# Reordering the first forty microseconds of a two-layer attention block on one core: norms, halves of x, values and queries, and the loads of the biases

## The chip, the core and the metric

The kernel runs on one core of one Trainium2 chip. The metric is the device time of one execution, in microseconds (us); lower is better. All arithmetic that matters is in float32. Matrix products are made from pairs of numbers, a high part (type fp32r) and a low part that holds the rest, with three matmuls for each product: high by high, high by low and low by high.

## What is computed

There are 32 sequences of 128 tokens with 512 features. Two layers of the same form run one after the other, each on the output of the one before. In short, for each sequence:

```
xn = layernorm(x) * norm_scale + norm_bias
q, k, v = xn @ Wq + bq, xn @ Wk + bk, xn @ Wv + bv      # 512 x 512 weights
k, v = masked(k), masked(v)
q = softmax(q, over the features of a head)             # 16 heads, then 8
k = softmax(k, over the tokens)
y = q @ (k.T @ v)                                       # linear attention, by head
scale, shift = split(silu(cond) @ W_film + b_film)
h = layernorm(y) * film_scale + film_bias, times (1 + scale), plus shift
x = x + silu(h) @ Wo + bo
```

## The kernel before

The x of all 32 sequences stays on chip (tile X, one slot of 128x512 for each sequence). A "tile" below is one sequence in one layer, so there are 64 of them; two neighbours, tiles 2g and 2g+1, are a pair g. Every engine has its own hand-written list of steps, which it works through strictly in order, and each step starts with waits on semaphores that other engines' steps raise. After the first few tiles the lists become a loop over tiles, step(s); the order of the steps before it is written out call by call, and the change is in that part alone. The calls that it touches:

- Weights. A 512x512 matrix is loaded in four chunks of 128 rows. `split_high(w, [c])` on ScalarE (ACT) copies chunk c of weight w into the high part; `split_low(eng, w, [c])` subtracts to get the low part (L346), on VectorE (DVE) or on GpSimd (POOL) depending on whose list it stands in. Weights 0 to 3 are Wk, Wv, Wq and Wo of the first layer. `keys(0)`, `values(0)` and `queries(0)` on TensorE (PE) wait chunk by chunk for these low parts.
- Norms. `stat_x(n)` on DVE takes mean and variance of tile n (L1515, L1518) and waits for the load of X where tile n is the first of a load. `root_x(n)` on POOL makes the reciprocal root. `norm_x(n)` on DVE (for tiles 0 to 3) writes the normalised tile XN (L1526).
- Turning. `turn_x(m)` on PE transposes half of the features of a pair (m = 2g + half) into PSUM; its first half waits for both tiles of the pair. `x_turned(m)` on ACT takes it out with the norm's scale and bias (two instructions at L935) and makes the high part XH (L942). `x_low(m)` makes the low part XL (L1563). The scale and bias lie in VC, which `start_vectors` on DVE copies (L1778) from what `turn_vectors` on PE transposed.
- Products. `keys(i)`, `values(i)`, `queries(i)` on PE are 24, 12 and 12 matmuls (L1152). Each waits until DVE has emptied the PSUM bank of the tile before: `queries(1)` waits for the first instruction of DVE's `queries(0)` (L1608), `values(1)` for DVE's `values(0)` (L1620). DVE's `queries(i)` also takes the maximum by head (L1612); then POOL's `queries(i)` subtracts it (L658), and then DVE's `turn_queries(i)` turns the result into QS (L1547).
- Filling. `keep_busy(b, n)` on PE makes n products of the identity with itself that nobody reads; each shows as two instructions in the profile.
- Loads. SyncE (SP) issues the large loads one after the other into one queue: `load_x(n)` (load 2 is tiles 2 and 3, load 3 tiles 4 to 7, load 4 tiles 8 to 11), `load_w(w)` (1 MB), `load_bias(r)` (a row of 512 numbers for all 128 partitions; 0 is bv, 1 bq, 2 bo) and `load_film(n)` (2 MB). `wait_split(1)` holds SP until the low parts of Wv are made, since load 4 goes into the place where Wv was staged.

Later in the opening, after DVE's `stat_x(5)` and `stat_x(6)`, DVE's list goes on with `start()`, `start_cond()` (L1756), `x_low(2)`, `x_low(3)`, `start_valid()` (L1748, L1749). PE's `turn_cond()` waits for `start_cond()`, PE's `count()` (L1351) for `start_valid()`, and `keys(2)` stands behind both.

Of the kernel before, what the change touches and what calls it, by code (L numbers as in the profile page):

```python
# [44 lines left out]
def build_blocks(nc, x, cond, mask0, mask1, weights, film_w, vec_rows, bias_rows, out):  # L45
# [21 lines left out]
    with ctx:  # L67
# [84 lines left out]
        B_K, B_V, B_Q, B_XK, B_O, B_TY, B_Y = 0, 1, 2, 3, 4, 5, 6  # L152
# [63 lines left out]
        def placed_x(g):  # L216
            return 16 * Q * ((g - FIRST) // 2 + 1)
# [123 lines left out]
        def split_low(eng, w, chunks):  # L341

            for c in chunks:
                wait_weights(eng, w, c)
                eng.wait_ge(act_w, C * w + c + 1)
                eng.tensor_tensor(WL[w % 4][:, c, :], STAGES[w][:, c, :], WH[w % 4][:, c, :].bitcast(F32),  # L346
                                  ALU.subtract).then_inc(low_w[w][c], 1)
# [26 lines left out]
        def _(eng):  # L374
# [4 lines left out]
            def load_w(w):  # L379
                src = weights[0][w].rearrange("(c p) n -> p c n", p=P)  # L380
                eng.dma_start(STAGES[w][:, :, :], src).then_inc(ld_w[w - 1], 16)
# [17 lines left out]
            def load_bias(r):  # L399
                eng.dma_start(BB[:, r, :], bias_rows[r:r + 1].partition_broadcast(P)).then_inc(ld_bias[r], 16)  # L400
# [101 lines left out]
            load_first(eng, [1])  # L502
            load_x(2)
            load_w(1)
            load_bias(2)
            load_bias(0)
            load_bias(1)
            load_w(2)
            load_film(0)
            load_x(3)  # L510
            wait_split(1)
# [89 lines left out]
        def _(eng):  # L601
# [16 lines left out]
            def root_x(n):  # L618
                eng.wait_ge(dve_stat, n + 1)
                r = n % RING  # L620
                if n - RING >= 2 * FIRST:
                    eng.wait_ge(act_xn, n - RING - 2 * FIRST + 1)
                if n < 2 * FIRST:
                    root(MVX[:, r, 1:2], VEX[:, :], RSX[:, r:r + 1]).then_inc(pool_x, 1)
                else:
                    root(MVX[:, r, 1:2], VEX[:, :], RSX[:, r:r + 1]).then_inc(pool_own, 1)
                    own[0] += 1
                    eng.wait_ge(pool_own, own[0])
                    eng.tensor_scalar(NBX[:, r:r + 1], MVX[:, r, 0:1], RSX[:, r:r + 1], -1.0, ALU.mult, ALU.mult)\  # L629
                       .then_inc(pool_x, 1)  # L630
                eng.wait_ge(pool_x, n + 1)
# [62 lines left out]
            mask_of_keys(0)  # L694
            root_x(2)
            root_x(3)
            split_low(eng, 2, [0])
            normalise_keys(0)
            queries(0)
# [112 lines left out]
        def _(eng):  # L812
            def split_high(w, chunks=range(C)):

                if w in LAST_USE:
                    eng.wait_ge(LAST_USE[w], B)
                for c in chunks:
                    wait_weights(eng, w, c)
                    eng.activation(WH[w % 4][:, c, :], STAGES[w][:, c, :], ACT.Copy).then_inc(act_w, 1)
# [98 lines left out]
            def x_turned(m):  # L918

                g, p = divmod(m, 2)  # L920
                l = g // (B // 2)
                if g < FIRST:
                    eng.wait_ge(pe_a, m + 1)
                elif p == 0:
                    eng.wait_ge(ld_xt[g % 2], placed_x(g))
                if g == 0 and p == 0:
                    eng.wait_ge(dve_vec, 1)
                wait_x_low(eng, m - 1 if m <= 2 * FIRST else m)
                xf = XF1 if m in (1, 3) else XF0[:, :, :]
                for cc in range(2):  # L930
                    if g < FIRST:
                        src = PS[:, B_X[p], cc * PAIR:(cc + 1) * PAIR].rearrange("p (t q n) -> p t q n", t=2, q=Q)
                    else:
                        src = XT[:, :, :, 2 * p + cc, :].rearrange("p q t n -> p t q n")
                    f = eng.activation(xf[:, cc, :].rearrange("p (t q n) -> p t q n", t=2, q=Q), src, ACT.Identity,  # L935
                                       bias=vec(l, "norm_bias", 2 * p + cc, 1),
                                       scale=vec(l, "norm_scale", 2 * p + cc, 1))
                f.then_inc(act_xf, 1)
                eng.wait_ge(act_xf, m + 1)
                if g >= 2:  # L940
                    eng.wait_ge(pe_q, 2 * g - 2)
                eng.activation(XH[g % 2][:, 2 * p:2 * p + 2, :], xf, ACT.Copy).then_inc(act_xh, 1)  # L942
# [24 lines left out]
            eng.dma_start(MI, mask0).then_inc(ld_mask, 16)  # L967
            eng.dma_start(MF, mask1).then_inc(ld_mask, 16)
            split_high(0, [0])
            split_high(0, [1])  # L970
            split_high(0, [2])
            split_high(0, [3])
            x_turned(0)
            x_turned(1)
            split_high(1, [0])
            split_high(1, [1])
            cond_tanh()
# [160 lines left out]
        def _(eng):  # L1138
            def bank(b, a=0, n=512):
                return PS[:, b, a:a + n]  # L1140
# [43 lines left out]
            def values(i):  # L1184
                eng.wait_ge(dve_v, i)
                project_x(i, 1, bank(B_V), pe_v)
# [109 lines left out]
            def turn_x(m):  # L1296
                g, p = divmod(m, 2)
                if m >= 2:
                    eng.wait_ge(act_xf, m - 1)
                for t in range(2):  # L1300
                    if p == 0:
                        eng.wait_ge(dve_xn, m + t + 1)
                    for cc in range(2):
                        f = (2 * p + cc) * P
                        mm = eng.transpose(bank(B_X[p], cc * PAIR + t * T, T), XN[:, t, f:f + P], ident[:, :])
                mm.then_inc(pe_a, 1)
# [29 lines left out]
            def turn_vectors():  # L1336

                eng.wait_ge(pool_const, 4)
                eng.wait_ge(ld_vec, 16)
                n = 2 * VROWS  # L1340
                eng.transpose(bank(B_TY, 0, n), VR, ident[0:n, 0:n]).then_inc(pe_vec, 1)

            def keep_busy(b, n):

                for _ in range(n):
                    eng.matmul(bank(b, 0, P), ident[:, :], ident[:, :], start=True, stop=True)
# [13 lines left out]
            def turn_valid():  # L1360

                eng.wait_ge(dve_mask_rows, 1)
                for l in range(2):
                    mm = eng.transpose(bank(B_O, (EC + l) * B, B), MT if l == 0 else MF, ident[0:B, 0:B])
                mm.then_inc(pe_valid, 1)

            eng.wait_ge(pool_const, 2)
            keep_busy(B_Q, 4)
            keep_busy(B_Q, 6)
            turn_x(0)  # L1370
            turn_vectors()
            turn_x(1)
            keep_busy(B_Q, 2)
            keep_busy(B_Q, 2)
            keep_busy(B_Q, 2)
            keep_busy(B_Q, 2)
            keep_busy(B_Q, 2)
            keep_busy(B_Q, 2)
            keep_busy(B_Q, 2)
            keys(0)  # L1380
            keys(1)
            keep_busy(B_Q, 2)
            turn_x(2)
            turn_valid()
            queries(0)
            values(0)
            queries(1)
            turn_x(3)
            values(1)
            turn_cond()  # L1390
            count()
            keys(2)
# [107 lines left out]
        def _(eng):  # L1500
# [20 lines left out]
            def norm_x(n):  # L1521
                g, t = divmod(n, 2)
                eng.wait_ge(pool_x, n + 1)
                if g > 0:
                    eng.wait_ge(pe_a, 2)
                eng.tensor_scalar(XN[:, t, :], X[:, n % B, :], MVX[:, n % RING, 0:1], RSX[:, n % RING:n % RING + 1],  # L1526
                                  ALU.subtract, ALU.mult).then_inc(dve_xn, 1)
# [55 lines left out]
            def key_sums(i):  # L1583

                eng.wait_ge(act_ek, i + 1)
                eng.wait_ge(pool_kn, i)
                eng.reciprocal(RE[:, :], SE[:, i % 2, :]).then_inc(dve_re, 1)  # L1587
# [187 lines left out]
            def start_vectors():  # L1775

                eng.wait_ge(pe_vec, 1)
                eng.tensor_copy(VC[:, :], PS[:, B_TY, 0:2 * VROWS]).then_inc(dve_vec, 1)  # L1778

            stat_x(0)  # L1780
            stat_x(1)
            norm_x(0)
            split_low(eng, 0, [0])
            norm_x(1)
            split_low(eng, 0, [1])
            split_low(eng, 0, [2])
            start_vectors()
            split_low(eng, 0, [3])
            stat_x(2)
            stat_x(3)  # L1790
            x_low(0)
            x_low(1)
            split_low(eng, 1, [0])
            start_masks()
            norm_x(2)
# [2 lines left out]
            keys(0)  # L1798
            split_low(eng, 2, [1])
            split_low(eng, 2, [2])  # L1800
            split_low(eng, 1, [3])
            split_low(eng, 2, [3])
            split_low(eng, 1, [1])
            keys(1)
            key_sums(0)
            queries(0)
            stat_x(4)
            values(0)
            turn_queries(0)
            stat_x(5)  # L1810
            stat_x(6)
# [232 lines left out]
```

## Time and profile before

| what | value |
|---|---|
| time, median of 3 executions | 863.16 us (862.21 to 863.73) |
| span of the profiled execution | 861.2 us |
| median less that span (what lies around the profiled instructions) | 1.96 us |
| busy PE, PE weight load, DVE, ACT, POOL | 98%, 84%, 79%, 70%, 64% |

The profile gives the start and length of every instruction of one execution, in us from the start of its span. Of an engine's list it shows what ended an idle time (in brackets, behind an arrow). The chain of work that ended last is followed back from the last instruction: at each step to what released it, or to the instruction ahead of it on its engine. DMA rows give the time from issue to landing. The granted clock (PEclk) is the share of TensorE's full speed, 1.00 for 2.4 GHz and 0.50 for 1.2 GHz.

### The profile page before, as it was taken

Reading aid. Unit: us, or ns where it says so; the run is one execution under the profiler, and the core shown is the slowest. Engines: PE = TensorE matmul, PEld = TensorE weight load, DVE = VectorE, ACT = ScalarE, POOL = GpSimd, SP = SyncE. Lnnn points to the kernel's source line nnn. Section 1 sums busy time; section 2 is a strip of 40 time slices with the busy share of each in tenths; the row PEclk is TensorE's granted clock in tenths of the full one; section 3 lists DMA queues with packets and bytes.
Section 4 is the critical chain, followed back from the end, with each engine's and each line's share of the span. In section 5 each row is a group of like instructions: output and inputs, shape, how many; then the busy total and the mean of one; then the engine's idle time right before and its main releaser. Section 6 shows DMA issues by size and latency. Waiting matters only on the chain.

```text
span 861.2 us, 20095 instructions
## 1 busy us (share of the span) xinstructions
PE 842.2 (98%) x6659; PEld 720.4 (84%) x6659; DVE 679.9 (79%) x1362; ACT 602.7 (70%) x1442; POOL 548.8 (64%) x741
## 2 busy tenths in 40 slices
PE   7999999999999999999999999999999999999998
PEld 7778888888888888888877888888888888888886
DVE  6987778778788778778887887778778777787666
ACT  5377677677676776677777786776676676676665
POOL 3467765765765756766767767667667656765641
PEclk8999999999999999999999999999999999999999
DMA  9876676776776766656578656656566655667441
GB/s 304 286 221 207 190 230 189 226 226 192 201 216 197 227 208 185 178 167 180 168 232 235 194 176 185 208 181 203 167 197 199 201 187 185 177 192 206 145 159 62
DMA packets 139404, 169.81 MB, mean 197 GB/s; under 512 B 12302, under 2 KB 112006, under 8 KB 139302
## 3 DMA queue, kind: packets, MB, share of 16 engines
q1 hardware_dynamic: 138512, 167.56, 64.0%
q8 instruction: 53, 0.87, 0.4%
q10 hardware_dynamic: 790, 0.98, 0.4%
q14 instruction: 49, 0.40, 0.2%
HBM read 95.61 MB, written 72.88 MB: 196 GB/s over the span
## 4 chain that ended last, share of the span: by engine, by line
PE 76%; DMA 9%; DVE 4%; SPq 3%; issue 3%; ACT 3%; POOL 2%; DVEq 0%; ACTq 0%; POOLq 0%
PE PS L1152 65%; PE PS L1248 6%; PE PS L1232 3%; DMA k_turned<-KT 2%; DMA X<-in_x 2%; DMA QT<-qy_turned 2%; DMA EK<-k_turned 1%; DMA qy_turned<-QS 1%; SPq L438 1%; DMA XT<-x_turned 1%; SPq L459 1%; PE PS L1322 1%; ACT Z L867 1%; POOL XL L667 1%; ACT XF L935 0%
## 5 line engine op out<-in xcount | busy, mean ns | idle before, releaser
L680 POOL TENSOR_TENSOR HL<-H,HH 128x512 fp32r<-128x512 f32 x60 | 77.4, 1290 | 190.1 <-ACT HH L916 190.0
L867 ACT ACTIVATE Z<-QT,FC,FA 128x128 f32<-128x128 f32 x240 | 99.0, 483 | 92.0 <-DMA QT<-qy_turned 92.0
L1152 PE MATMUL PS<-XH,WH_k 128*128 128x256 f32 x512 | 149.7, 292 | 0.7 <-DVE KN L1581 0.7
L1152 PE MATMUL PS<-XH,WL_k 128*128 128x256 f32 x512 | 144.7, 283 | 0.0
L1152 PE MATMUL PS<-XL,WH_k 128*128 128x256 f32 x512 | 144.7, 283 | 0.0
L953 ACT ACTIVATE XN<-X,NBX,RSX 128x512 f32<-128x512 f32 x60 | 48.8, 813 | 86.6 <-POOL NBX L629 86.6
L829 ACT ACTIVATE SK<-SK,KN 128x128 f32<-128x128 f32 x256 | 98.9, 388 | 11.2 <-DVE KN L1581 11.2
L1152 PE MATMUL PS<-WH_o,HH 128*128 128x512 f32 x248 | 102.3, 413 | 3.4 <-issue 3.2
L1152 PE MATMUL PS<-WH_q,XH 128*128 128x512 f32 x256 | 100.7, 394 | 0.0
L1152 PE MATMUL PS<-WH_v,XH 128*128 128x512 f32 x256 | 100.7, 394 | 0.0
L1152 PE MATMUL PS<-WL_v,XH 128*128 128x512 f32 x256 | 100.3, 392 | 0.0
L1152 PE MATMUL PS<-WL_q,XH 128*128 128x512 f32 x256 | 99.8, 390 | 0.0
L1152 PE MATMUL PS<-WH_q,XL 128*128 128x512 f32 x256 | 99.7, 389 | 0.0
L1152 PE MATMUL PS<-WH_v,XL 128*128 128x512 f32 x256 | 99.6, 389 | 0.0
L1152 PEld LDWEIGHTS PS<-XH,WH_k 128*128 128x128 f32 x512 | 97.8, 191 | 1.3 <-issue 1.1
L1152 PE MATMUL PS<-WL_o,HH 128*128 128x512 f32 x248 | 98.1, 395 | 0.0
L1152 PEld LDWEIGHTS PS<-XL,WH_k 128*128 128x128 f32 x512 | 97.9, 191 | 0.1
L1152 PE MATMUL PS<-WH_o,HL 128*128 128x512 f32 x248 | 98.0, 395 | 0.0
L1152 PEld LDWEIGHTS PS<-XH,WL_k 128*128 128x128 f32 x512 | 97.8, 191 | 0.0
L651 POOL TENSOR_TENSOR X<-X,BB 128x512 f32<-128x512 f32 x64 | 83.7, 1309 | 0.2
L667 POOL TENSOR_TENSOR XL<-XF,XH 128x512 fp32r<-128x512 f32 x60 | 78.1, 1301 | 5.5 <-issue 4.2
L674 POOL TENSOR_TENSOR SK<-SK,RE 128x512 f32<-128x512 f32 x64 | 66.6, 1041 | 19.6 <-DVE RE L1587 19.4
(171 smaller groups left out, 2108.3 us busy)
## 6 DMA issues: line engine op xcount, KB each, us to landing
qy_turned<-QS SPq DMA_DIRECT2D x60, 512.0 KB, 2.9
QT<-qy_turned SPq DMA_DIRECT2D x240, 128.0 KB, 3.1
EK<-k_turned SPq DMA_DIRECT2D x128, 128.0 KB, 2.8
x_turned<-XS SPq DMA_DIRECT2D x30, 512.0 KB, 3.3
XT<-x_turned SPq DMA_DIRECT2D x120, 128.0 KB, 3.5
k_turned<-KT SPq DMA_DIRECT2D x52, 256.0 KB, 3.9
out_x<-X SPq DMA_DIRECT2D x31, 256.0 KB, 3.3
X<-in_x SPq DMA_DIRECT2D x11, 512.0 KB, 5.3
```

The source lines that it names most:

```text
L438: eng.dma_start(QT[32 * fq:32 * fq + 32, :, 0:n, :, :].rearrange("p q h c n -> p q (h c n)"), src[fq])\
L459: eng.dma_start(EK[32 * tq:32 * tq + 32, :, :, :, :, :].rearrange("p f h t c n -> p f (h t c n)"), src[tq])\
L651: eng.tensor_tensor(X[:, b, :], X[:, b, :], BB[:, 2, :], ALU.add).then_inc(pool_bo, 1)
L667: eng.tensor_tensor(XL[g % 2][:, dst, :], XF0[:, :, :], XH[g % 2][:, dst, :].bitcast(F32), ALU.subtract).then_inc(pool_xl, 1)
L674: eng.tensor_tensor(sk, sk, RE[:, :].unsqueeze(2).to_broadcast([P, 4, T]), ALU.mult).then_inc(pool_kn, 1)
L680: eng.tensor_tensor(hl_of(o), h_of(o), hh_of(o).bitcast(F32), ALU.subtract).then_inc(pool_hl, 1)
L829: e = eng.activation(SK[:, p, a, :], SK[:, p, a, :], ACT.Exp, bias=KN[:, p, t, cc:cc + 1], accum_out=SE[:, p, a:a + 1])
L867: z = eng.activation(z_of(o)[:, c * P:c * P + P].rearrange("p (q n) -> p q n", q=Q), src, ACT.Identity, bias=FC[l][:, c, b:b + 1], scale=F ...
L953: eng.activation(XN[:, t, :], X[:, n % B, :], ACT.Identity, bias=NBX[:, r:r + 1], scale=RSX[:, r:r + 1]).then_inc(act_xn, 1)
L1152: mm = eng.matmul(dst, left[a](c), right[b](c), start=(c == 0 and a + b == 0), stop=(c == C - 1 and a == 1))
L1232: mm = eng.matmul(PS[f:f + 32, bank_att(j), c * P + a:c * P + a + w], vs if l == 0 else ks, ks if l == 0 else vs, start=True, stop=True, t ...
L1248: mm = eng.matmul(bank(B_Y + c // 2, (c % 2) * W, W), EQ[:, c * P:c * P + P], ATT[:, c // 2, (c % 2) * W:(c % 2 + 1) * W], start=True, sto ...
```

## The change

No step is added or removed except fillers of PE; steps stand at other places of the lists, and two low parts move from DVE to POOL.

- SP: Wq is loaded ahead of the three biases, and these come in the order bv, bq, bo (before: bo, bv, bq, then Wq).
- POOL: chunks 1 and 3 of Wv's low part are made here, ahead of Wq's chunk 0.
- ACT: `x_turned(0)` follows the first chunk of Wk and `x_turned(1)` the second (before: both after all four).
- PE: `turn_vectors()` comes before `turn_x(0)`; `values` come before `queries` for tiles 0 and 1, and `turn_x(3)` comes after `values(1)`; ahead of `keys(0)` 9 filler products stand where 14 stood, and the 2 after `keys(1)` are gone.
- DVE: `start_vectors` and `norm_x(1)` come ahead of the first low part of Wk; `x_low(0)`, `x_low(1)` and `stat_x(2)` come between its chunks; two chunks of Wv are gone; and the order behind `key_sums(0)` is `values(0)`, `stat_x(4)`, `queries(0)` (before: `queries(0)`, `stat_x(4)`, `values(0)`).

```diff
@@ SP
             load_w(1)
-            load_bias(2)
+            load_w(2)
             load_bias(0)
             load_bias(1)
-            load_w(2)
+            load_bias(2)
             load_film(0)
             load_x(3)
@@ POOL
             root_x(3)
+            split_low(eng, 1, [1])
+            split_low(eng, 1, [3])
             split_low(eng, 2, [0])
@@ ACT
             split_high(0, [0])
+            x_turned(0)
             split_high(0, [1])
+            x_turned(1)
             split_high(0, [2])
             split_high(0, [3])
-            x_turned(0)
-            x_turned(1)
@@ PE
             eng.wait_ge(pool_const, 2)
-            keep_busy(B_Q, 4)
-            keep_busy(B_Q, 6)
+            keep_busy(B_Q, 10)
+            turn_vectors()
             turn_x(0)
-            turn_vectors()
             turn_x(1)
-            keep_busy(B_Q, 2)
...
+            keep_busy(B_Q, 9)
             keys(0)
             keys(1)
-            keep_busy(B_Q, 2)
             turn_x(2)
+            values(0)
             turn_valid()
             queries(0)
-            values(0)
+            values(1)
+            turn_x(3)
             queries(1)
-            turn_x(3)
-            values(1)
             turn_cond()
@@ DVE
             norm_x(0)
+            start_vectors()
+            norm_x(1)
             split_low(eng, 0, [0])
-            norm_x(1)
+            x_low(0)
             split_low(eng, 0, [1])
+            stat_x(2)
+            x_low(1)
             split_low(eng, 0, [2])
-            start_vectors()
             split_low(eng, 0, [3])
-            stat_x(2)
             stat_x(3)
-            x_low(0)
-            x_low(1)
             split_low(eng, 1, [0])
...
             split_low(eng, 2, [2])
-            split_low(eng, 1, [3])
             split_low(eng, 2, [3])
-            split_low(eng, 1, [1])
             keys(1)
             key_sums(0)
+            values(0)
+            stat_x(4)
             queries(0)
-            stat_x(4)
-            values(0)
             turn_queries(0)
```

## Rows read from the trace of the kernel before

**Rows 1.** The page: busy time by engine, then the whole chain by engine.

```profile
PE 842.2 (98%) x6659; PEld 720.4 (84%) x6659; DVE 679.9 (79%) x1362; ACT 602.7 (70%) x1442; POOL 548.8 (64%) x741
...
PE 76%; DMA 9%; DVE 4%; SPq 3%; issue 3%; ACT 3%; POOL 2%; DVEq 0%; ACTq 0%; POOLq 0%
```

**Rows 2.** The chain in order of time, 18 to 60: start, length, what.

```profile
10.84 18.50 DMA X<-in_x
...
29.37 0.70 DVE BNX L1515
...
30.92 0.70 DVE QS L1547
...
35.40 0.81 DVE XL L1563 x2
...
36.86 0.41 PE PS L1351 x2
37.26 2.95 PE PS L1152 x24
40.22 1.85 PE PS L1322 x16
42.07 8.56 PE PS L1152 x48
```

**Rows 3.** Timeline of PE: start, length, line, count, idle before and its releaser.

```profile
9.16 0.69 PE L1305 MATMUL PS<-ident,XN 128*128 128x128 f32 x2 [2.41 <-DVE XN L1526]
...
16.10 0.36 PE L1152 MATMUL PS<-XH,WH_k 128*128 128x256 f32 x1
...
34.40 0.39 PE L1152 MATMUL PS<-WH_v,XL 128*128 128x512 f32 x1
35.46 0.68 PE L1357 MATMUL PS<-ident,XS 32*128 32x32 f32 x8 [0.67 <-DVE XS L1756]
```

**Rows 4.** Timeline of DVE, 0 to 45.

```profile
8.57 0.54 DVE L1526 TENSOR_SCALAR XN<-X,MVX,RSX 128x512 f32<-128x512 f32 x1
...
12.35 0.68 DVE L1515 BATCH_NORM_STATS2 BNX<-X 128x6 f32<-128x512 f32 x1
...
20.90 1.15 DVE L1581 TENSOR_TENSOR KN<-VC,KB 128x4 f32<-128x4 f32 x1
21.98 1.28 DVE L346 TENSOR_TENSOR WL_q<-X,WH_q 128x512 fp32r<-128x512 f32 x2
...
26.82 0.69 DVE L1608 TENSOR_TENSOR SQ<-PS,BB 128x512 f32<-128x512 f32 x1
27.55 0.69 DVE L1612 TENSOR_REDUCE QM<-SQ 128x16 f32<-128x512 f32 x1
29.37 0.69 DVE L1515 BATCH_NORM_STATS2 BNX<-X 128x6 f32<-128x512 f32 x1 [1.13 <-DMA X<-in_x]
...
30.31 0.69 DVE L1620 TENSOR_TENSOR VV<-PS,BB 128x512 f32<-128x512 f32 x1
```

**Rows 5.** Timeline of POOL, 0 to 50.

```profile
20.71 1.32 POOL L346 TENSOR_TENSOR WL_q<-X,WH_q 128x512 fp32r<-128x512 f32 x1 [5.05 <-ACT WH_q L819]
...
28.32 1.05 POOL L658 TENSOR_TENSOR SQ<-SQ,QM 128x512 f32<-128x512 f32 x1 [0.33 <-DVE QM L1612]
```

**Rows 6.** Timeline of ACT, 0 to 50.

```profile
11.93 1.02 ACT L935 ACTIVATE XF<-PS,VC 128x256 f32<-128x256 f32 x2 [0.78 <-DVE VC L1778]
...
19.91 2.19 ACT L819 ACTIVATE WH_q<-X 128x512 fp32r<-128x512 f32 x4 [1.60 <-DMA X<-in_wq]
```

**Rows 7.** Stretches: their length, busy time by engine, granted clock, DMA share, GB/s.

```profile
5.10:8.50 3.40, 1.07 (x8) 0.64 (x6) 1.45 (x4) 1.55 (x2) 1.41 (x3) 1.00 0.88 226
8.50:15.30 6.80, 6.13 (x28) 5.70 (x29) 5.26 (x12) 4.97 (x10) 2.78 (x5) 0.50 1.04 347
12.00:25.00 13.00, 13.00 (x91) 12.49 (x90) 11.45 (x22) 11.31 (x27) 3.33 (x5) 0.87 1.05 386
34.70:37.10 2.40, 1.01 (x11) 0.82 (x11) 2.40 (x7) 1.31 (x5) 0.00 (x0) 1.00 0.99 366
```

More of the change, by code:

```diff
@@ L1367, in _ @@
             eng.wait_ge(pool_const, 2)
-            keep_busy(B_Q, 4)
-            keep_busy(B_Q, 6)
+            keep_busy(B_Q, 10)
+            turn_vectors()
             turn_x(0)
-            turn_vectors()
             turn_x(1)
-            keep_busy(B_Q, 2)
-            keep_busy(B_Q, 2)
[L1375 to L1379, printed above, removed]
+            keep_busy(B_Q, 9)
             keys(0)
             keys(1)
-            keep_busy(B_Q, 2)
             turn_x(2)
+            values(0)
             turn_valid()
             queries(0)
-            values(0)
+            values(1)
+            turn_x(3)
             queries(1)
-            turn_x(3)
-            values(1)
             turn_cond()
```

## Prediction

> **What bounds the kernel now.** I read the page first. PE is busy for 98% of the span and is 76% of the chain that ended last, with DMA 9% and DVE 4% [rows 1]. So the loop is PE's, and what happens in the opening reaches the end only by the moment at which PE comes to its unbroken work. The second view is the chain in order of time around the change [rows 2]. It does not run over the first products at all. It starts from load 3 of x (tiles 4 to 7), issued at 10.84 and landed 18.50 later, at 29.34. DVE's `stat_x(4)` waits for it, and from there the chain stays on DVE, through `values(0)`, `turn_queries(0)` (QS, 30.92), two more statistics, `start()`, `start_cond()`, `x_low(2)` and `x_low(3)` (35.40) and `start_valid()`, until PE's `count()` at 36.86. Then PE works without a gap, `keys(2)` from 37.26 and on to 50.63. The third view, the timelines, shows the same from the other side: DVE sat idle for 1.13 ahead of 29.37 and for nothing visible after it [rows 4], while PE, done with its first products at 34.40 + 0.39 = 34.79, waited 0.67 for `start_cond()` [rows 3].
>
> Two prices follow from these rows. 24 matmuls of 256 columns take 2.95. The 48 matmuls that take 8.56 are one `keys`, one `queries` and one `values`, so 12 matmuls of 512 columns take (8.56 - 2.95) / 2 = 2.8 [rows 2].
>
> **Part 1, everything up to the landing of load 3: about 2 us earlier, worth nothing by itself.** Before, `norm_x(1)` stood behind a low part, at 8.57 [rows 4], and PE's second half of `turn_x(0)` waited 2.41 for it [rows 3]. `x_turned(0)` waited for VC until 11.93 [rows 6]. Both waits go. What is late next is `stat_x(2)`, now ahead of `x_low(1)`. It ran at 12.35 [rows 4], and its load is issued as before, so I leave it there. Behind it stand 0.9 of statistics, `x_low(1)` and two low parts at 0.64 each (1.28 for two [rows 4]): 12.35 + 0.9 + 3 x 0.64 = 15.2. From then the last chunk of the first half of `keys(0)` and its second half remain, 15 of 24 matmuls, 1.8: ended at 17.0, against 16.10 + 2.95 = 19.05 [rows 2, 3]. If PE's clock falls in the pause ahead of 15.2, as it did before (0.50 from 8.50 to 15.30 [rows 7]), this is nearer 18 to 19. The removed fillers ran at that low clock and beside this wait, so they cost nothing and bring nothing.
>
> `values(0)` then needs Wv's low parts. POOL makes two of them at 1.32 each [rows 5] where DVE took 0.64. Wq's high parts waited 1.60 for their load [rows 6]. It now lands ahead of three biases of 0.26 MB, at 386 GB/s [rows 7] 2.0 us sooner. Low parts on both engines can collide: a subtraction of four numbers on DVE took 1.15 while POOL made a low part, from 20.71 to 22.03 [rows 4, 5]. Two more on POOL can hold DVE for at most 2 x 1.32 = 2.6.
>
> Does DVE still reach `stat_x(4)` in time? Ahead of it DVE loses two low parts (1.28) and `queries(0)` (0.73 + 0.69 = 1.42), and gains `values(0)` (0.69 at most). With the 1.13 that it was idle, that is 3.1 of room, against at most 2.6 of new collisions. So DVE waits for load 3 in any case, and all that was gained before 29.34 ends in that wait.
>
> Load 3 itself I leave at 29.34. The same bytes stand ahead of it in the same queue, and from 12 to 25 the DMA engines were full (share 1.05 [rows 7]). Load 4 is issued sooner, since Wv's low parts are ready sooner, but behind load 3. I give this term 0.4 either way. The Trainium skill (DMA: Bandwidth & Descriptors, Queues, rings and completion order) says that each engine consumes the descriptors of a ring in their order; by that, changed places ahead of load 3 can't move it.
>
> **Part 2, behind the landing: +2.0 us.** This is where the change costs. `stat_x(4)` ends as before, and the next DVE step can start at 30.31 [rows 4]. That was `values(0)`, and `turn_queries(0)` followed at 30.92 [rows 2], since POOL had finished with its input at 28.32 + 1.05 = 29.37 [rows 5]. Now the next step is `queries(0)`, and `turn_queries(0)` needs POOL in between:
>
> - first instruction of `queries(0)`: 30.31, and 0.73 to the next (26.82 to 27.55 [rows 4]): 31.04
> - maximum by head, 0.69 [rows 4]: 31.73
> - to POOL, from 28.24 (27.55 + 0.69) to 28.32, 0.08, and 1.05 there [rows 4, 5]: 32.86
> - back to DVE, 0.07, taken like the step to POOL: 32.93
>
> against 30.92, so 2.0 later. DVE stands idle for 1.2 of it with its whole list queued behind. `turn_queries(0)`'s list neighbours don't change, DVE had no idle time from there to `count()`, and so `start_cond()`, `x_low(3)` and `start_valid()` shift by 2.0, and `keys(2)` on PE from 37.26 to 39.27. SP's store of these queries and the second film load behind it shift by the same. PE was unbroken from there on, and the chain runs over it, so the whole shift reaches the end.
>
> The other moves at this place cost nothing. `queries(1)` on PE now waits for `queries(0)`'s first instruction, at 31.0. It ends at 31.05 + 2.8 = 33.85, still 3.6 before `start_cond()` is there. `turn_x(3)` and ACT's `x_turned(3)` come a little earlier than before.
>
> **Part 3, PE's clock: +1.5 us.** PE will stand still from 33.85 to 35.46 + 2.0 = 37.47, then work 0.68 (`turn_cond`), wait about 0.7, and work 0.41 (`count`) until `keys(2)`: 1.1 of work in 5.3. The nearest row is the stretch from 5.10 to 8.50: with 1.07 of work in 3.40 the granted clock then fell from 1.00 (2.4 GHz) to 0.50 (1.2 GHz) and stayed there until 15.30, though PE was busy for 6.13 of those 6.80 [rows 7]. The row that speaks against it is 34.70 to 37.10: with 1.01 of work in 2.40 the clock held [rows 7]. The coming pause is longer and emptier than both, so I take the fall as likely. Its price: at half the clock, work of a length t at the low clock costs about t/2. From below 0. From above, the low clock lasts for 6.1 of work as it did then, 3.0. Part of the low time will lie in the pause itself, so I take the middle, 1.5. It falls on `keys(2)` and what follows, where PE is the chain.
>
> The Trainium skill (TensorE: Matmul & The Clock Gate, Part 1 and HAM oscillation) says that the low clock is the default which only activity lifts, and that bursts of matmuls parted by waits start cold each time. By this rule the time is the forecast's; without it, it is the first rival's.
>
> **The sum.** In the profiled execution, 861.2 + 2.0 + 1.5 = 864.7. The median lies 1.96 above that span: 863.16 + 3.5 = 866.7.
>
> **Rivals.**
>
> - The clock holds in the pause: 863.16 + 2.0 = 865.2. For it the stretch 34.70 to 37.10, against it the one before 8.50 [rows 7]. Chance 0.18.
> - Not slower, because load 3 lands earlier. The forecast turns at this: each 1 us by which load 3 lands before 29.34 takes 1 us off, down to where DVE is ready, about 26.6 by the count above. Zero lies at 27.3; at 26.6 the gain is 2.7 - 2.0 = 0.7, PE's pause shrinks with it and the clock holds: 862.4. For it only that issues are moved; against it the full DMA engines. Chance 0.08.
> - The early gain carries: if DVE's list is not what `keys(2)` waits for, the 2.0 of Part 1 comes off: 861.1. Against it speak all of rows 2. Chance 0.07.
> - The order is later and the shift is half swallowed, because in the steps after `keys(2)` PE waits for something which doesn't move, such as a load: 1.0 or less stays, 864.0. Against it: PE unbroken until 50.63 [rows 2]. Chance 0.12.
> - The low clock lasts as long as the first time, or falls once more: 868.2 or more. Chance 0.08.
>
> The forecast has 0.47.
>
> **The numbers.** About 0.2%, 1.7 us, is what a measurement of this kernel can tell from no change: 861.4 to 864.9. Faster: the third rival and a little, 0.08. Within: the second and fourth, and the near edge of the first, 0.24. Slower: 0.68. The range from 862.8 to 868.8 takes in the forecast, the first and fourth rival, half of the last, and the 0.4 of load 3; it leaves out the third rival and most of the second.
>
> **What the profile after would show.** `keys(0)` ends between 17 and 19 and PE is through `values(0)` before 25 (Part 1). DVE is idle for more than 1.13, up to 3, in front of a `stat_x(4)` that still starts near 29.4. Then `queries(0)` at 30.3, an idle time of about 1.2 that POOL's L658 ends, and QS at 32.9 (Part 2). `keys(2)` starts near 39.2, and the granted clock is 0.50 over part of 37 to 43 (Part 3). I am wrong if `stat_x(4)` starts well before 29, if QS comes before 32, or if the distance from `keys(2)` to the end of the span shrinks.

## The result, and the profile after

The changed kernel is slower. Beside the kernel before it takes 869.39 us (867.45 to 870.47, 6 executions) against 862.42 us (860.95 to 863.73, 6), a ratio of 1.0067 with a 95% interval of 1.0049 to 1.0085. A second measurement, given below, has 867.21 against 863.38 and a ratio of 1.0050 (1.0030 to 1.0070). By the ratios that is 5.8 and 4.3 us. (The recorded ratio is not the quotient of the two medians, which is 1.0081 in the first measurement.) Executions of one kernel scatter by up to 5 us on either side of their median in this work, and the two intervals overlap between 4.2 and 6.0 us.

The page of the changed kernel, again busy time and the chain by engine (as [rows 1]):

```profile
span 868.7 us, 20069 instructions
PE 844.6 (97%) x6645; PEld 720.7 (83%) x6645; DVE 680.7 (78%) x1360; ACT 602.4 (69%) x1442; POOL 552.8 (64%) x743
...
PE 80%; DMA 8%; DVE 4%; SPq 3%; issue 3%; POOL 1%; ACT 1%; DVEq 0%; ACTq 0%; POOLq 0%
```

The engines do the same work; the span is 7.5 us longer. DVE's timeline (as [rows 4]) shows the place:

```profile
17.74 1.60 DVE L1520 TENSOR_SCALAR XN<-X,MVX,RSX 128x512 f32<-128x512 f32 x1 [0.47 <-POOL RSX L616]
19.27 1.78 DVE L346 TENSOR_TENSOR WL_v<-X,WH_v 128x512 fp32r<-128x512 f32 x1
...
26.31 0.69 DVE L1614 TENSOR_TENSOR VV<-PS,BB 128x512 f32<-128x512 f32 x1
29.11 0.69 DVE L1509 BATCH_NORM_STATS2 BNX<-X 128x6 f32<-128x512 f32 x1 [2.11 <-DMA X<-in_x]
...
30.05 0.69 DVE L1602 TENSOR_TENSOR SQ<-PS,BB 128x512 f32<-128x512 f32 x1
30.78 0.69 DVE L1606 TENSOR_REDUCE QM<-SQ 128x16 f32<-128x512 f32 x1
32.63 0.71 DVE L1541 STREAM_TRANSPOSE QS<-SQ 128x512 f32<-128x512 f32 x1 [1.16 <-POOL SQ L658]
```

DVE waits 2.11 for load 3 (before: 1.13). Then it does `queries(0)`, waits 1.16 for POOL, and `turn_queries(0)` (QS) starts at 32.63 instead of 30.92 [rows 2]: 1.71 late. PE's timeline (as [rows 3]), and behind it the chain in order of time (as [rows 2]):

```profile
14.60 0.38 PE L1154 MATMUL PS<-XH,WH_k 128*128 128x256 f32 x1 [2.89 <-DVE WL_k L346]
...
37.16 1.06 PE L1359 MATMUL PS<-ident,XS 32*128 32x32 f32 x8 [3.23 <-DVE XS L1750]
38.56 0.64 PE L1353 MATMUL PS<-VALID,H 128*128 128x32 f32 x2 [0.35 <-DVE VALID L1743]
```

```profile
39.20 4.62 PE PS L1154 x24
43.81 1.85 PE PS L1324 x16
...
91.81 1.11 issue
92.93 3.03 PE PS L1154 x12
```

PE stands still for 3.23 ahead of `turn_cond`. `keys(2)` comes at 39.20, 1.94 after the 37.26 of before, and takes 4.62 instead of 2.95, 1.67 longer. So the 16 matmuls of the film weights start at 43.81 against 40.22 [rows 2]: 3.59 behind. The stretches tell why (columns as in [rows 7]):

```profile
36.20:42.90 6.70, 5.40 (x28) 5.26 (x29) 5.68 (x13) 0.00 (x0) 3.09 (x7) 0.50 0.90 338
469.60:472.90 3.30, 3.30 (x36) 2.64 (x27) 1.74 (x3) 2.25 (x4) 2.64 (x2) 0.50 0.83 291
```

The granted clock was 0.50 over these 6.7 us, from within the pause to 0.9 before the end of `keys(2)`. The second row is another fall, at the change of layers, which the profile of before did not have.

The other 3.9 of this execution's 7.5 arose later, bit by bit. Two of the places, first before, then after (timelines of ACT and PE):

```profile
81.13 1.65 ACT L867 ACTIVATE Z<-QT,FC,FA 128x128 f32<-128x128 f32 x4 [1.76 <-DMA QT<-qy_turned]
...
462.67 0.65 PE L1232 MATMUL PS<-VV,EK 128*32 128x64 f32 x32 [1.35 <-DMA EK<-k_turned]
```

```profile
86.24 1.65 ACT L869 ACTIVATE Z<-QT,FC,FA 128x128 f32<-128x128 f32 x4 [2.68 <-DMA QT<-qy_turned]
...
469.35 0.96 PE L1234 MATMUL PS<-VV,EK 128*32 128x64 f32 x32 [2.02 <-DMA EK<-k_turned]
```

The read-back of turned queries comes 5.1 late at 86.24, 1.5 more than PE was behind at 43.81; PE stands still for 1.11 at 91.81. At the change of layers PE waits 2.02 for a DMA instead of 1.35, the shift is 6.7, and then the second low clock adds to it.

A second execution of the same kernel, profiled later, had neither the late read-back nor the second low clock (1.00 from 469.6 to 472.9; its DMA wait there was 1.79), and its span was 865.3. Its opening was another too:

```profile
28.37 0.69 DVE L1509 BATCH_NORM_STATS2 BNX<-X 128x6 f32<-128x512 f32 x1 [1.37 <-DMA X<-in_x]
...
31.89 0.71 DVE L1541 STREAM_TRANSPOSE QS<-SQ 128x512 f32<-128x512 f32 x1 [1.16 <-POOL SQ L658]
38.46 5.07 PE PS L1154 x24
43.53 1.85 PE PS L1324 x16
```

(two rows of DVE's timeline, two of the chain). Load 3 landed 1.0 earlier than in the kernel before, so QS was only 0.97 late and `keys(2)` 1.20, but `keys(2)` took 2.12 longer, and the film matmuls were again 3.3 behind.

Followed over the whole span, by the start of each tile's product of ATT and EQ (L1248 before, L1250 after), the two executions were behind the kernel before by this much:

| time in the kernel before | 52.6 | 90.7 | 168 | 285 | 452 | 466 | end |
|---|---|---|---|---|---|---|---|
| first | +3.6 | +5.1 | +5.8 | +6.8 | +6.1 | +8.2 | +7.5 |
| second | +3.4 | +3.4 | +4.5 | +3.9 | +3.7 | +4.1 | +4.1 |

So the opening's shift is carried on, and on top of it the distance to another execution wanders by up to 2 us at a time.

### The profile page after: what moved, and what is told of

The parts are those of the page before. It is cut to its first block, busy times and chain, and to the rows that moved or that the text cites. A ratio compares the mean times of both kernels' runs of the same rounds, so it can differ in the third digit from the quotient of the medians.

```text
span 868.7 us, 20069 instructions
## 1 busy us (share of the span) xinstructions
PE 844.6 (97%) x6645; PEld 720.7 (83%) x6645; DVE 680.7 (78%) x1360; ACT 602.4 (69%) x1442; POOL 552.8 (64%) x743
## 4 chain that ended last, share of the span: by engine, by line
PE 80%; DMA 8%; DVE 4%; SPq 3%; issue 3%; POOL 1%; ACT 1%; DVEq 0%; ACTq 0%; POOLq 0%
PE PS L1154 69%; PE PS L1250 6%; PE PS L1234 3%; DMA X<-in_x 2%; DMA k_turned<-KT 2%; DMA qy_turned<-QS 1%; DMA EK<-k_turned 1%; DMA QT<-qy_turned 1%; SPq L459 1%; PE PS L1324 1%; SPq L400 1%; DMA XT<-x_turned 1%; SPq L438 1%; POOL HL L680 0%; DVE BNX L1509 0%
## 5 line engine op out<-in xcount | busy, mean ns | idle before, releaser
L1154 PE MATMUL PS<-XH,WH_k 128*128 128x256 f32 x512 | 151.5, 296 | 4.0 <-DVE WL_k L346 2.9
```

The costliest lines, as they stand in the source:

```text
L1154: mm = eng.matmul(dst, left[a](c), right[b](c), start=(c == 0 and a + b == 0), stop=(c == C - 1 and a == 1))
```

## The experiments

Each is compared with executions of the kernel before on the same chip. "At the film matmuls" is how much later than 40.22 [rows 2] the 16 matmuls of `conditioning(0)` start in the profiled execution; it sums the order's shift, the clock's price in the opening and what load 3 landed earlier or later. "At the end" is the span of the same execution less the 861.2 of before. The medians are of 12 executions each (the changed kernel: 6), and of 17 to 35 of the kernel before (6 in the first row).

| kernel | median, us | less the kernel before | ratio (95%) | at the film matmuls | at the end |
|---|---|---|---|---|---|
| changed kernel, first | 869.39 | +6.97 | 1.0067 (1.0049 to 1.0085) | +3.59 | +7.5 |
| changed kernel, second | 867.21 | +3.83 | 1.0050 (1.0030 to 1.0070) | +3.31 | +4.1 |
| queries(0) ahead of stat_x(4) | 866.43 | +3.29 | 1.0031 (1.0016 to 1.0046) | -0.64 | +0.1 |
| values first, alone | 866.32 | +3.18 | 1.0032 (1.0017 to 1.0046) | +4.15 | +1.7 |
| changed, late pause filled | 865.97 | +2.83 | 1.0031 (1.0016 to 1.0045) | +1.39 | +1.3 |
| changed, load 3 before film | 865.66 | +2.52 | 1.0026 (1.0012 to 1.0040) | +1.98 | +4.0 |
| early moves alone | 864.09 | +0.71 | 1.0014 (0.9997 to 1.0030) | +0.17 | +0.8 |
| changed, both pauses filled | 865.09 | +3.34 | 1.0029 (1.0013 to 1.0046) | +1.81 | +1.7 |
| early moves alone, pauses filled | 860.42 | -1.33 | 0.9976 (0.9958 to 0.9994) | +0.43 | -1.9 |
| queries(0) ahead, pauses filled | 861.30 | -2.08 | 0.9974 (0.9961 to 0.9988) | -1.64 | -3.6 |
| load 3 early, statistics ahead | 862.94 | -0.44 | 1.0010 (0.9993 to 1.0027) | -1.3 | +0.7 |
| before, pauses filled | 861.25 | -0.50 | 0.9986 (0.9967 to 1.0004) | +0.12 | -1.9 |
| before, filled, pure delay of 2 us | 865.96 | +0.15 | 1.0015 (0.9993 to 1.0038) | +3.63 | +2.6 |

The last two columns are of one execution each, against one execution of the kernel before. Their difference runs from -2.5 to +3.9 and is 0.0 in the mean of the 13. So a single execution says little about how a shift of the opening ends, and all together say that it is neither enlarged nor swallowed as a rule.

**The changed kernel again.**

> The changed kernel itself once more, beside the experiments on the same chip. Times of one kernel scatter by some 3 us on either side here, so the experiments need it as their measure. Expected from the first measurement: 5 to 7 us over the kernel before. The experiments so far (each 2.5 to 3.3 us over the kernel before) give back half of that only if this one is again at 5 or more.

It came out at 3.8 over (4.3 by the ratio), under what was expected. So the first measurement had the loss rather large, and what the first group of experiments gave back is less certain for it. The mean granted clock of the whole execution was 0.992 in four of the first six executions and in one of the second six: the first had more low clock, and only for the profiled one of them is it shown where.

**One swap: queries(0) ahead of stat_x(4).**

```diff
             values(0)
-            stat_x(4)
             queries(0)
+            stat_x(4)
             turn_queries(0)
```

> The changed kernel with one swap: on VectorE queries(0) comes ahead of stat_x(4), so in the idle time ahead of load 3 and not behind its landing. Theory (the order behind the landing costs 1.9 us, and PE's low clock in the pause that it makes another 1.7): PE ends queries(0) at 28.2 as in the changed kernel, VectorE is through it at 29.7, GpSimd at 30.9, turn_queries(0) starts at 30.9 as in the kernel before, keys(2) at 37.3 with the granted clock at 1.00, and the time is that of the kernel before within 1 us. Rival (the early moves cost, such as GpSimd's low parts or the low clock from 15.6 to 19.0): keys(2) is still at 38 or later and at least 4 us of the loss stay.

The profiled execution is what the theory says:

```profile
28.38 0.69 DVE L1606 TENSOR_REDUCE QM<-SQ 128x16 f32<-128x512 f32 x1
28.98 0.68 DVE L1509 BATCH_NORM_STATS2 BNX<-X 128x6 f32<-128x512 f32 x1
...
30.28 0.71 DVE QS L1541
36.63 2.95 PE PS L1154 x24
```

(two lines of DVE's timeline, two of the chain). DVE does `queries(0)` while load 3 is on its way, QS is 0.6 earlier than before, `keys(2)` too and at full clock, and this execution took 863.12. But the median is 866.43, where the kernel before within 1 us was expected. Theory and rival each had a part right: the order is mended, and something else stayed. The executions told what to try. Of the twelve, the three with a mean granted clock of 0.998 or more took 863.1 to 863.9, the nine with less 865.2 to 869.1. Where the clock was low in those nine, no profile shows.

**The order of values and queries alone.**

```diff
@@ PE of the kernel before
+            values(0)
             turn_valid()
             queries(0)
-            values(0)
+            values(1)
+            turn_x(3)
             queries(1)
-            turn_x(3)
-            values(1)
@@ DVE of the kernel before
+            values(0)
+            stat_x(4)
             queries(0)
-            stat_x(4)
-            values(0)
             turn_queries(0)
```

> The kernel before with only values put ahead of queries for tiles 0 and 1, on VectorE (values(0), stat_x(4), queries(0)) and on PE (values(0), queries(0), values(1), turn_x(3), queries(1)); all early moves and the loads stay as before. Theory: turn_queries(0) starts at 32.9 and keys(2) at 39.2, 2.0 later than before; PE gets to values(0) only when Wv's last low part is there (25.1), so it ends queries(1) near 35.5, its pause is under 2 us, the clock holds, and the time is 2.0 us over the kernel before. If the steps behind amplify any shift, it is 4 or more over. Rival (the early moves cost): the time is that of the kernel before.

3.2 over the kernel before. `turn_queries(0)` started at 33.57, for another reason than I had expected: PE, with `values(0)` held up by Wv's low parts, brought `queries(0)` late. And the clock did not hold: PE's pause was only 1.31 and yet `keys(2)` took 4.44 (with pauses of 1.29 in the swap above and of 1.36 in the early moves alone, below, it took 2.95). So the new order costs without any of the early moves too, but this is no clean measure of how much.

**Fillers in the late pause.**

```diff
             queries(1)
+            keep_busy(B_K, 12)
             turn_cond()
```

> The changed kernel with 12 filler products of PE between queries(1) and turn_cond, about 2.7 us of work in the pause of 3.2. If the clock's fall there costs what the trace shows on keys(2) (4.62 against 2.95), the clock stays at 1.00, keys(2) takes 2.95 again and the time is 1.7 us under the changed kernel, still some 2 to 5 over the kernel before. If the clock matters nothing because something else is late next, the time is that of the changed kernel.

The clock stayed at 1.00, and in the chain `keys(2)` took 2.94 instead of 4.62:

```profile
38.67 2.94 PE PS L1154 x24
41.61 1.85 PE PS L1324 x16
```

Against the kernel before, its median is 2.8 over, where the changed kernel was 3.8 and 7.0 over; 1.7 less was expected. In the profile the clock's part is shown directly (here the clock held ahead of `keys(0)` as well); in the median the direction is right and the size within the scatter.

**Load 3 ahead of the film weights.**

```diff
-            load_film(0)
             load_x(3)
+            load_film(0)
```

> The changed kernel with load 3 (tiles 4 to 7) issued ahead of the first film weights, 2 MB, so that it lands some 5.4 us earlier, near 24. Theory: VectorE does not wait at stat_x(4), does it at 27.0 and is in queries(0) when PE has ended it at 28.2; turn_queries(0) starts at 30.9 to 31.0, keys(2) at 37.3, and the time is within 1 us of the kernel before. Rival (the landing of load 3 is not what sets keys(2)): the time is that of the changed kernel. The film weights land near 29 and are wanted at 40, so they cost nothing.

DVE no longer waited at `stat_x(4)` (26.71), but PE, whose clock was at 0.50 from 13.7 to 20.5 in this execution and from 15.6 to 19.0 in the changed kernel's, brought `queries(0)` only for 28.81, QS came at 31.39, and the clock fell just ahead of `keys(2)` all the same (4.39). So 1.24 of the 1.71 by which QS was late went, the clock's price stayed, and the median is 2.5 over, where less than 1 was expected.

**The early moves alone.** The changed kernel with the old order of values and queries on PE and DVE.

> The changed kernel with the old order of values and queries of tiles 0 and 1 on VectorE and PE; the early moves, the loads and the fillers stay as changed. Theory (the early moves end in the wait for load 3): turn_queries(0) and keys(2) are where they were in the kernel before, within 0.5 us, and the median is that of the kernel before within 1 us. Rival (the early moves cost by themselves, by the low clock or by another phase against the DMAs): 2 us or more over the kernel before, as the experiment with only queries(0) moved ahead of stat_x(4) was, whose keys(2) came 0.6 early and whose median was yet 3.3 over.

No difference that this measurement can tell (0.9997 to 1.0030). All that was won before 29 ended in a wait of 1.93 for load 3.

**Both pauses filled, in three orders.** 26 filler products stand ahead of `keys(0)` instead of 9, and 6 or 12 ahead of `turn_cond`:

```diff
-            keep_busy(B_Q, 9)
+            keep_busy(B_Q, 26)
             keys(0)
...
+            keep_busy(B_K, 6)
             turn_cond()
```

With queries(0) ahead of stat_x(4):

> The changed kernel with queries(0) ahead of stat_x(4) as before in the first experiment, and with PE's pauses filled: 26 filler products instead of 9 ahead of keys(0), and 6 between queries(1) and turn_cond. In the first experiment the three runs with a granted clock of 0.998 and more took 863.5, the nine below 865.2 to 869.1. If the clock is what the rest of the loss is, this one has no low clock in the opening and comes out at the kernel before or 0.5 under it. If it stays 2 us or more over, the rest is not the clock.

With the changed order (12 instead of 6):

> The changed kernel with its order as it is and both pauses of PE filled (26 fillers ahead of keys(0), 12 between queries(1) and turn_cond), so that only the order's cost is left: turn_queries(0) 1.0 to 2.0 later than in the kernel before (as load 3 lands), keys(2) the same, and a median 1.5 to 2.0 over the kernel before. If it is at 3 or more over, something else than the clock and that order costs; if at 0, the order costs nothing without the clock.

With the old order of values and queries:

> The early moves alone (old order of values and queries of tiles 0 and 1) with the same fillers: 26 ahead of keys(0), 6 ahead of turn_cond. With the clock held, all that the early moves win ends in the wait for load 3: keys(2) within 0.5 us of the kernel before and a median within 0.7 us of it. Against this kernel, the one with queries(0) ahead of stat_x(4) and the same fillers has only the order in its favour; it should then be 1.5 to 2 us faster.

The profiled executions of all three were at 1.00 throughout the opening. DVE in the first, the second and the third:

```profile
28.28 0.69 DVE L1510 BATCH_NORM_STATS2 BNX<-X 128x6 f32<-128x512 f32 x1 [0.23 <-DMA X<-in_x]
...
29.27 0.71 DVE L1542 STREAM_TRANSPOSE QS<-SQ 128x512 f32<-128x512 f32 x1
```

```profile
29.23 0.69 DVE L1510 BATCH_NORM_STATS2 BNX<-X 128x6 f32<-128x512 f32 x1 [2.39 <-DMA X<-in_x]
...
32.75 0.71 DVE L1542 STREAM_TRANSPOSE QS<-SQ 128x512 f32<-128x512 f32 x1 [1.16 <-POOL SQ L658]
```

```profile
29.81 0.69 DVE L1510 BATCH_NORM_STATS2 BNX<-X 128x6 f32<-128x512 f32 x1 [1.35 <-DMA X<-in_x]
...
31.36 0.70 DVE L1542 STREAM_TRANSPOSE QS<-SQ 128x512 f32<-128x512 f32 x1
```

With the clock out of play the order alone separates them: 2.1 under, 3.3 over and 1.3 under the kernel before. The changed order costs, clock or no clock. (Expected were 0 to 0.5 under, 1.5 to 2.0 over and at most 0.7 off.) Between it and the old order, measured on one chip, the medians are 4.7 apart, while the film matmuls are 1.4 apart (2.0 if load 3 had landed at one time in both: it came 0.6 later in the old order's execution). Why the distance is more than that of the opening stays open.

`queries(0)` ahead of the load is not shown to be better than the old order. QS came 2.1 earlier (29.27 against 31.36), but load 3 had landed 1.5 earlier in that execution; counted from the start of `stat_x(4)`, QS follows after 0.99 against 1.55, so the order gives 0.56. The medians (ratios 0.9974 and 0.9976, on two chips) show no difference, where 1.5 to 2 was expected.

The kernel with queries(0) ahead and the pauses filled is faster than both kernels of this case. Its order is that of the one swap, which was 3.3 over (on another chip, each against the kernel before there): fillers for a PE that waits anyway made some 5 us there. In the changed order they made less, 0.5 by the medians and 1.8 by the ratios of the second measurement and the filled one, and these runs do not show why.

**An attempt to beat both.** The changed kernel with load 3 first, `stat_x(5)` and `stat_x(6)` ahead of `turn_queries(0)`, and 26 fillers.

> An attempt to beat both: the changed kernel with load 3 ahead of the film weights, stat_x(5) and stat_x(6) ahead of turn_queries(0) on VectorE, where they cover GpSimd's part of queries(0), and 26 fillers ahead of keys(0). VectorE has no idle time left there: turn_queries(0) at 31.5, start_cond at 33, keys(2) at 35.2 to 35.8, 1.5 to 2 before the kernel before. If a shift of keys(2) reaches the end whole, the median is 1.5 to 2 under the kernel before; if the steps behind set the time, it is that of the kernel before or over it.

`keys(2)` came 1.3 earlier, less than expected, and the median is that of the kernel before. In the profiled execution the gain was lost near 62, where PE waited for ACT and the clock then fell:

```profile
62.68 1.97 PE L1250 MATMUL PS<-ATT,EQ 128*128 128x132 f32 x8 [2.29 <-ACT EQ L849]
```

**Fillers in the kernel before, and a pure delay.**

```diff
-            keep_busy(B_Q, 6)
+            keep_busy(B_Q, 20)
             turn_x(0)
...
+            keep_busy(B_K, 3)
             turn_cond()
```

> The kernel before with PE's pauses of the opening filled: 14 more filler products ahead of turn_x(0), so that PE works through until XN of tile 1 is there at 9.1, and 3 between values(1) and turn_cond. Nothing else is changed. Theory (in the kernel before, the low clock from 8.5 to 15.3 lies beside waits and costs nothing): the median is that of the kernel before within 1 us, with granted clocks of 0.998 to 1.0. If fillers by themselves give what the kernel with both pauses filled gave (2.1 us under the kernel before), this one is 2 under as well, and the order has no part in that gain.

Fillers alone gave 0.5, no more than the scatter (0.9967 to 1.0004). That fits a low clock of before, from 8.5 to 15.3 [rows 7], that lay beside waits. To this kernel a delay of DVE was added, and 11 fillers in place of 3:

```diff
             values(0)
+            stall(5)
             turn_queries(0)
```

> The kernel before with PE's pauses filled, and nothing else but a pure delay of VectorE: five small reductions (0.4 us each, written to a place that is written again later) ahead of turn_queries(0), so that this and all behind it comes 2.0 us later; the fillers ahead of turn_cond are 11 instead of 3. The changed kernel with its pauses filled had keys(2) 1.8 later than the kernel before and a median 3.3 over it, and stood 4.7 over the early moves with fillers, whose keys(2) was 0.4 late. If a shift of the opening is carried to the end as it is, this one is 2.0 over the filled kernel before, so 1.0 to 1.5 over the kernel before. If the steps behind enlarge any such shift, it is 3 or more over the kernel before, and the excess of the changed order needs no cause of its own.

The delay is there, and the clock fell in spite of the fillers:

```profile
30.95 2.07 DVE L1745 TENSOR_REDUCE FOLD<-ident 128x32 f32<-128x128 f32 x5
33.05 0.71 DVE L1548 STREAM_TRANSPOSE QS<-SQ 128x512 f32<-128x512 f32 x1
```

```profile
37.58 0.67 PE L1357 MATMUL PS<-ident,XS 32*128 32x32 f32 x8 [0.91 <-DVE XS L1762]
38.98 0.53 PE L1351 MATMUL PS<-VALID,H 128*128 128x32 f32 x2 [0.73 <-DVE VALID L1755]
```

The kernel before was slower on this chip than on the others (median 865.81, 860.8 to 868.5), and the ratio of 1.0015 (0.9993 to 1.0038) is 1.3 us over it, within the 1.0 to 1.5 expected of a shift that is carried as it is. The interval, -0.6 to 3.3 us, reaches from no cost to the 3 of the other reading, so it only leans against the thought that the steps behind enlarge every shift. The delay was not pure either: with the fall of the clock the film matmuls came 3.63 late in the profiled execution, and its span was 2.6 over.

## Why the prediction was right, and where its size was off

I had forecast 866.7, 3.5 over. The direction, the place and the mechanism hold; the first measurement's 869.39 lies 0.6 above my range of 862.8 to 868.8, the second, 867.21, within it. By the ratios the loss was 5.8 and 4.3, so the forecast was low both times.

- **Part 1, nothing by itself: right.** `keys(0)` ended at 18.5 at the low clock, as written for that case (18 of its matmuls were left at 14.60, not the 15 that I had counted), `values(0)` at 24.8. DVE waited 2.11 for load 3. The early moves alone make 1.0014, no difference. Low parts on both engines did collide: with two of them running on POOL, DVE's norm took 1.60 (0.54 in [rows 4]) and a low part 1.78 (0.64). It stayed under the room that I had counted. The Trainium skill (SBUF — State Buffer, Who interferes with whom) says that a DVE instruction with two SBUF inputs and a GpSimd one that reads SBUF exclude each other; the trace agrees, with 1.78 for that low part.
- **Load 3: right in the first execution, in part by luck.** It landed at 29.09, 0.25 early, within the 0.4 given. In the second it landed 1.0 early. By the start of `stat_x(4)`, wherever DVE waited for it with the load in its old place, it was there between 28.3 and 29.8; 0.4 was too narrow.
- **Part 2, +2.0: right.** From the start of `stat_x(4)` to QS it is 3.52 in all four profiled executions that have the changed order and wait for load 3, and 1.55 or 1.56 in the four that have the old order and no delay: 1.97 for the order, whenever the load lands. QS came 1.71 late, since the load was 0.25 early; POOL's wait was 1.16 of the 1.2. `keys(2)` was 1.94 late. With no low clock the changed order kept +1.8 at the film matmuls against +0.4 for the old one. Moving `queries(0)` ahead of the wait takes the shift away: -0.64, and -1.64 with fillers, where 1.1 of it is load 3, which landed earlier than before in that execution.
- **Part 3, +1.5: right in the profile, too small a view of the clock.** The fall came in the pause and cost 1.67 on `keys(2)`, and 2.12 in the second execution. (The pause with its work is 5.4 by the numbers of the prediction, not 5.3; nothing hangs on it.) The Trainium skill (TensorE: Matmul & The Clock Gate, HAM oscillation) has the stretch after a gap start cold, and the trace agrees: 4.62 for `keys(2)` where the filled pause had 2.94. What I had missed is how little it takes. I had the row of 34.70 to 37.10 [rows 7] as a sign that short pauses are safe. Yet the clock fell after pauses of 1.31 (values first alone) and of 0.91 and 0.73 (pure delay). It held after 1.36 (early moves alone) and after 1.29 (the one swap), but nine of the swap's twelve executions had a lower mean clock than the profiled one.
- **The step that fell short is the last: "the whole shift reaches the end" as the whole of it.** At the film matmuls the changed kernel was 3.59 behind, against the 3.5 of my sum. The end was 7.5 behind in that execution, and 4.1 in the other profiled one (865.3 against 861.2). In the first, 1.5 came by 90.7, with a later DMA read-back near 86, 1.7 more by 285, and 2.1 between 452 and 466, where a longer wait for a DMA was followed by a second low clock; 1.4 of all this went again. The second execution had neither the read-back's 1.5 nor the second low clock, so these belong to the execution, although four of the first six had a mean clock as low as the profiled one's. Over all 13 profiled executions the shift arrives unchanged in the mean (0.0, from -2.5 to +3.9). So the step holds as a mean, and no spread was given for it. Whether the changed order costs more than its shift in the opening stays open: with both pauses filled it is 1.8 at the film matmuls, 3.3 by the medians and 2.5 by the ratio, whose interval (1.1 to 4.0 us) holds 1.8 as well.

Of the rivals, "the low clock lasts longer, or falls once more" (868.2 or more, 0.08) is nearest to the first measurement, and in its profile the clock did fall once more; it deserved more than 0.08. "The clock holds" had 2.0 over the kernel before; the filled changed order has 3.3 by the medians and 2.5 by the ratio, which agrees within the interval. That its 865.09 is so near that rival's 865.2 is luck, since the kernel before was at 861.75 on that chip.

## What to carry to other kernels

Where an engine waits for a transfer, look at what stands behind the wait in its list: here a step that needs a second engine's answer was moved from the idle time ahead of the load to behind it, and its 1.4 us and the other engine's 1.1 became the path, while the early work that was sped up only made the wait longer. A pause of TensorE costs more than its length when the clock falls in it, and fillers in it are cheap to try: they turned one order that measured 3.3 us over into one at 2.1 under, though they gave the changed order only 0.5 to 1.8. Where executions differ by 3 us and more, one profile is a sample, and several are wanted, with their granted clocks. What stays the same in all of them, here the 3.52 and 1.55 from the landing to QS, is the better measure of an order.

## What the runs showed that I had not expected

- The same kernel seems to keep the clock in one execution and to lose it in another: of twelve executions with queries(0) ahead of stat_x(4), three had a mean clock of 0.998 or more, nine between 0.992 and 0.996, and their mean times were 863.5 and 866.9. The 3.4 between them is what 0.004 less of mean clock makes of 861 us. With the pauses filled, ten of twelve were at 1.00.
- The clock fell with pauses of under 1 us on either side of 0.67 us of work (the pure delay, above).
- The column of the granted clock says 1.00 for the first 5 us, but the filler matmuls there are no faster than those at 0.50 (in the kernel before 4.2 us for 20 against 5.4 us for 28 from 11.0 on, most of it at 0.50; in the changed one 2.2 us for 18 from 8.1 on at 1.00).
